# Two graph layers on one core: TensorE's register loads per couple of spans, and one branch per couple

## The chip, the core and the metric

The program runs on one core of a Trainium2 chip. The metric is the device time of that core in microseconds (us); the median over several executions is compared. Lower is better.

## The reference

There are 6250 nodes with 256 features, and 100000 edges sorted by their destination. The input is normalised per row, then two relational graph layers follow, a residual sum, a second normalisation and a mixture of 8 experts (top 2) with a residual sum. One graph layer is:

```
xs = x[src]
seg = dst * R + etype                          # R = 8 relations
sums = segment_sum(xs, seg, N * R)
mean = sums / max(cnt, 1)
out = x @ Wroot + b + einsum('nrd,rde->ne', mean.reshape(N, R, D), W)
```

The destinations are drawn as `6250 * u**2`, so the first nodes have many edges and the last ones few.

## The kernel before

**Blocks and spans.** The sorted edges are cut into 784 blocks of 128 edges. POOL gathers the source rows of one block per indirect DMA (L450) into a ring of 16 places, each with a high and a low half in float16 and a column of ones. The 49 tiles of 128 nodes are cut into 8 spans of 16 nodes (16 nodes x 8 relations = 128 rows of sums). Two spans are a couple, so a tile has 4 couples, numbered k = 0 to 3, and a layer has 196. The edges of a span touch at least one block; the program always takes two (its "first blocks") and, if they touch more, the further ones one by one.

**DVE** builds the 0/1 selection matrices: `sel` for the two first blocks of each span (L890), two couples ahead, and `sel_more` for every further block (L898), one couple ahead. It also takes the reciprocal of the counts (layer 0 alone), and the low halves of the means (L933). **ACT** writes the high halves of the means (L589) and copies transposed means out of PSUM (L561).

**TensorE** (PE) does, for every couple (function `couple`, L1258 and after), in this order: for both spans a wait for the rows and once for `sel`, then `add_block` (L1234, L1235: two matmuls each, high and low) for the two first blocks, then `more_sums` (L1237 to L1242: a branch, and if there are further blocks a loop over them, each with a wait for `sel_more`). Between these stand some of the products of the layer's weights with the means of the tile before (`product`, L1254, three matmuls a part, 18 parts a tile). At the end come 8 transposes of the means of the couple before (`turn`, L1246), which wait for DVE.

**What PE's sequencer does.** Where a block lies is known only on the chip. PE's own sequencer therefore loads numbers into registers and works out places and wait values from them. `load_meta` (L1225 to L1229) loads 20 numbers once a tile: first block and running count of further blocks, for 8 spans and a little more. The place of a block in the ring is `block & 15` and that is multiplied out to an address, for each matmul of `add_block`. A couple has two branches of its own (L1238), one per span, over the loop of further blocks.

```
1238                     with pe.If(upto > since):
1239                         with pe.Fori(0, upto - since) as i:
1240                             pe.wait_ge(more_ready[layer], since + i + 1)
```

**The order of the products.** A tile's 18 parts are spread over the couples k = 1, 2, 3 and the k = 0 of the next tile as 2, 6, 5 and 5. In k = 1 both stand at the couple's end, behind a wait for the last means of the tile (`means_in`).

**SyncE** (SP) passes on two kinds of events: a landed gather becomes `rows_ready` (L355), and a place in the ring of which PE has taken the last sum becomes `slots_free` (L362), for which POOL waits.

**Tiles.** `graph_tiles` writes out tiles 0, 1 and 48 and puts the others, in pairs, in a loop of 23 turns, so that on PE the code of 8 couples is the body of a loop (its backward branch is at L294). Behind the two layers, from about 2290 us on, comes the mixture of experts, which the change touches in nothing but the type of one small table.

## Time and profile before

| | |
|---|---|
| median of 3 runs | 3062.41 us (3062.01 to 3065.25) |
| the profiled execution: span, which is all of its own time that the page gives | 3064.4 us |
| PE busy | 2352.2 us (77%) |
| POOL busy | 1836.5 us (60%) |
| DVE busy | 1782.2 us (58%) |
| ACT busy | 1167.6 us (38%) |
| first and last tile of layer 0 begin on PE | 95.3 and 1174.2 us |
| first and last tile of layer 1 begin on PE | about 1197.1 and 2264.5 us |
| mean granted clock of TensorE | 0.879 |

"Busy" counts matmuls, copies and gathers. The instructions of a sequencer (register arithmetic, branches, loads of registers, semaphores) are not in it; they show as "issue", and with a q behind the engine's name (PEldq is PE's sequencer) in the view of one source line. A busy share of PE is no share of its peak, since the ends of matmuls overlap.

### The profile page before, as it was taken

To read this page: it belongs to the slowest core of one execution; us is meant where nothing else is said; L and a number is where in the kernel's file an instruction comes from. 1 tells how busy PE (TensorE), PEld (TensorE's weight loads), DVE (VectorE), ACT (ScalarE), POOL (GpSimd) and SP (SyncE) were. 2 spreads that over 40 slices of the span, in tenths; PEclk is the share of its full clock that TensorE was granted. 3 is DMA by queue.
4 is the path that set the end of the run, shared out by engine and by line. 5 is a ranking of instruction groups with operands and counts; after the bars stand their busy time and mean duration, and the time that the engine had idled before them with its cause. 6 is when DMAs were issued, how large, how long until landed. Compare 5 with 4: busy or idle time off the path is not lost.

```text
span 3064.4 us, 82720 instructions
## 1 busy us (share of the span) xinstructions
PE 2352.2 (77%) x19212; PEld 1776.0 (58%) x19213; DVE 1782.2 (58%) x4944; ACT 1167.6 (38%) x2306; POOL 1836.5 (60%) x1908
## 2 busy tenths in 40 slices
PE   1456777778888887456777888888987189999999
PEld 0123444555666775123445556667776178888888
DVE  7434445555566664333445555656666278877777
ACT  5001223334445553011223344455542165655554
POOL 1777777766666553777777777666536623333333
PEclk9556789999999998557899999999995599999999
DMA  7343333333333321333343444333335432322222
GB/s 244 100 130 105 108 108 108 109 101 99 97 94 93 90 88 58 106 99 115 115 119 118 123 122 125 112 113 111 106 110 192 146 123 86 100 72 72 72 72 61
DMA packets 164416, 331.14 MB, mean 108 GB/s; under 512 B 35518, under 2 KB 101786, under 8 KB 164216
## 3 DMA queue, kind: packets, MB, share of 16 engines
q0 software_dynamic: 90864, 245.38, 26.9%
q1 hardware_dynamic: 39608, 41.02, 4.5%
q10 hardware_dynamic: 33872, 43.92, 4.5%
q8 instruction: 27, 0.44, 0.1%
q14 instruction: 45, 0.37, 0.0%
HBM read 283.29 MB, written 49.07 MB: 108 GB/s over the span
## 4 chain that ended last, share of the span: by engine, by line
PE 48%; POOL 24%; issue 15%; DVE 7%; DMA 3%; DVEq 2%; ACT 1%; POOLq 0%; SPq 0%; ACTq 0%
POOL ring L450 20%; PE more_banks L1254 15%; PE sum_banks L1392 8%; PE sum_banks L1234 7%; PE sum_banks L1235 5%; PE sum_banks L1382 4%; PE more_banks L1382 4%; POOL lot_in L470 3%; PE more_banks L1246 3%; DMA ring<-table,row_tab 2%; DVE sel L890 1%; DMA out<-edge_work,lot_ids 1%; PE more_banks L1366 1%; DVEq L881 1%; DVE weights L1072 0%
## 5 line engine op out<-in xcount | busy, mean ns | idle before, releaser
L450 POOL DMA_INDIRECT ring<-table,row_tab x1568 | 1509.2, 963 | 703.8 <-issue 339.0
L1254 PE MATMUL more_banks<-weights,stage 128*128 128x256 f16 x5292 | 846.9, 283 | 7.8 <-ACT stage L561 4.5
L589 ACT ACTIVATE stage<-sum_banks,inv 128x256 f16<-128x256 f32 x784 | 327.4, 471 | 815.5 <-DVE inv L923 398.7
L1254 PEld LDWEIGHTS more_banks<-weights,stage 128*128 128x128 f16 x5292 | 502.4, 101 | 144.9 <-issue 71.6
L1234 PE MATMUL sum_banks<-ring,sel 128*128 x1568 | 449.3, 287 | 161.1 <-DVE sel L890 84.2
L898 DVE TENSOR_SCALAR sel_more<-lane,win_off,key_tab 128x128 f16 x780 | 268.8, 345 | 443.4 <-SPq L355 371.2
L1234 PE MATMUL sum_banks<-ring,sel_more 128*128 x780 | 244.3, 314 | 350.0 <-DVE sel_more L898 193.8
L890 DVE SCALAR_TENSOR_TENSOR sel<-lane,win_off,key_tab 128x256 f16<-128x256 f16 x792 | 349.4, 482 | 240.4 <-PE more_banks L1254 235.8
L1235 PE MATMUL sum_banks<-ring,sel 128*128 x1568 | 448.7, 287 | 0.0
L561 ACT ACTIVATE stage<-more_banks 128x1024 f16<-128x1024 f16 x392 | 402.7, 1027 | 15.1 <-PE more_banks L1246 14.9
L1234 PEld LDWEIGHTS sum_banks<-ring,sel_more 128*128 x780 | 78.4, 100 | 529.7 <-issue 524.9
L933 DVE SCALAR_TENSOR_TENSOR stage<-sum_banks,inv,stage 128x256 f16<-128x256 f32 x784 | 345.4, 479 | 25.8 <-issue 13.3
L1234 PEld LDWEIGHTS sum_banks<-ring,sel 128*128 128x128 f16 x1568 | 157.4, 100 | 266.5 <-issue 240.5
L489 POOL DMA_INDIRECT out<-edge_work,lot_ids x106 | 108.1, 1019 | 325.0 <-DVE edge_work L1160 308.7
L587 ACT ACTIVATE stage<-sum_banks 128x256 f16<-128x256 f32 x196 | 75.1, 383 | 591.3 <-DVE inv L923 302.1
L1235 PE MATMUL sum_banks<-ring,sel_more 128*128 x780 | 261.2, 336 | 0.0
L1246 PE MATMUL more_banks<-ident,stage 128*128 128x128 f16 x3136 | 257.3, 229 | 0.1
L665 ACT ACTIVATE stage<-sum_banks,edge_work,undo 128x256 f32<-128x256 f32 x212 | 113.0, 561 | 315.6 <-PE sum_banks L1382 294.1
L1246 PEld LDWEIGHTS more_banks<-ident,stage 128*128 128x128 f16 x3136 | 223.3, 103 | 14.0 <-DVE stage L933 1.2
L1392 PE MATMUL sum_banks<-weights,edge_work 128*128 128x256 f16 x1824 | 208.1, 275 | 7.5 <-DVE edge_work L1144 7.5
L920 DVE TENSOR_SCALAR inv<-sum_banks 128x2 f32 (+1 forms) x196 | 31.2, 159 | 290.6 <-PE more_banks L1254 276.1
L1392 PEld LDWEIGHTS sum_banks<-weights,edge_work 128*128 128x128 f16 x1824 | 179.5, 99 | 29.9 <-issue 8.4
(287 smaller groups left out, 2763.0 us busy)
## 6 DMA issues: line engine op xcount, KB each, us to landing
ring<-table,row_tab POOLq DMA_INDIRECT x1568
weights<-L_ffn_W ACTq DMA_DIRECT2D x96, 178.5 KB
stage<-L_ffn_W ACTq DMA_DIRECT2D x16, 1024.0 KB, 5.5
edge_work<-lot_in SPq DMA_DIRECT2D x54, 260.0 KB, 2.7
table<-edge_work SPq DMA_DIRECT2D x7, 896.0 KB, 4.4
table<-edge_work ACTq DMA_DIRECT2D x49, 128.0 KB
out<-acc SPq DMA_DIRECT2D x6, 1024.0 KB
acc<-x SPq DMA_DIRECT2D x6, 896.0 KB, 11.0
```

The lines of the kernel that those rows point to most:

```text
L450: pool.indirect_dma_start(ring_rows[:, b % RING, 0:2 * D], None, tables[layer], bass.IndirectOffsetOnAxis(row_tab[:, b:b + 1], 0)).then_in ...
L561: act.activation(means[:, par, :, :, 2 * k * WIN:(2 * k + 2) * WIN].rearrange("p q r (v n) -> p v (q r) n", v=2), ps_turn[slot].rearrange( ...
L589: act.activation(mean16[:, slot, h, 0:D], ps_sum[slot][h][:, 0:D], ACT.Copy, scale=inv[:, ds(c * 2 + h, 1)]).then_inc(mean_high[layer], 1)
L890: return v.scalar_tensor_tensor(sel[:, slot, h], lane16[:].unsqueeze(1).to_broadcast([P, 2, P]), win_off[:, ds(w, 1)], key_tab[:, ds(lo, 2 ...
L898: v.tensor_scalar(flat(sel_more[:, ds(block & (RING - 1), 1), :]), lane16[:], win_off[:, ds(w, 1)], key_tab[:, ds(block, 1)], ALU.add, ALU ...
L933: v.scalar_tensor_tensor(mean16[:, slot, h, D:2 * D], ps_sum[slot][h][:, 0:D], inv[:, ds(c * 2 + h, 1)], mean16[:, slot, h, 0:D], ALU.mult ...
L1234: pe.matmul(to[:, 0:D + 1], hot, flat(slot[:, :, D:2 * D + 1]), start=first, stop=last, skip_group_check=True)
L1235: return pe.matmul(to[:, 0:D], hot, flat(slot[:, :, 0:D]), start=False, stop=last, skip_group_check=True)
L1246: out = [pe.transpose(ps_turn[slot][:, (4 * h + q) * P:(4 * h + q + 1) * P], mean16[:, slot, h, q * P:(q + 1) * P], ident16[:]) for h in r ...
L1254: return [pe.matmul(ps_out[par], rows[:, xp * KD + k, :], w16[:, wp, k, r * D:(r + 1) * D], start=part == 0 and n == 0, stop=part == PARTS ...
L1382: ins = pe.matmul(hid_bank[c % 4], up_sb[slot][:, wp, k, c * P:(c + 1) * P], lotT[:, zp, k, :], start=k == 0 and (wp, zp) == PART_PAIRS[0] ...
L1392: ins = pe.matmul(bank[2 + h][:, 0:D], hidT[:, hp, c, h * P:(h + 1) * P], down_sb[slot][:, wp, c, :], start=c == 0 and (hp, wp) == PART_PA ...
```

## The change

TensorE no longer loads 20 numbers a tile. A new table `pe_row`, made once by DVE, holds six numbers per couple: for each span the two addresses in the ring of its first blocks, multiplied out, and in the two third places what the rows must have reached for both spans, and how many further blocks the couple has. PE loads these six at the start of every couple. If the couple has further blocks, a second load fetches six numbers of the old table, and an arm follows that does what was done before. Else a second arm does the first blocks of both spans with the products between, and has no further branch. The products are spread 5, 4, 4, 5 over k = 0 to 3, root parts first, and the wait for `means_in` moves from the end of k = 1 to the start of k = 2. On other engines: wait values that come from registers are masked (SP, DVE, PE), on ACT `relu_rows` comes from k = 2 to k = 3, before the transposed means, and on DVE `sums_out` goes from k = 1 to k = 2 and the bias sum from k = 2 to k = 1.

```diff
+    MASK = (1 << (BLOCKS + 3 * WINDOWS).bit_length()) - 1
+    PART_ORDER = [R * KD + k for k in range(KD)] + list(range(R * KD))
+    SHARES = (5, 4, 4, 5)
+    SPREAD = {4: (1, 1, 0, 1, 1), 5: (1, 1, 1, 1, 1)}
...
+        pe_row = sb("pe_row", [1, 6 * COUPLES], i32)
...
-                        sp.wait_ge(steps_done[layer], sp.snap(regs[s], donate=True, min_val=1, max_val=BLOCKS + 3 * WINDOWS))
+                        sp.wait_ge(steps_done[layer], sp.snap(regs[s], donate=True) & MASK)
...
+            for b in range(2):
+                link(v.tensor_scalar(places, lo, float(b), None, ALU.add))
+                link(v.tensor_scalar(places, places, RING - 1, None, ALU.bitwise_and))
+                link(v.tensor_scalar(pe_meta[0:1, :, :, b], places.rearrange("o (c h) -> o c h", h=2), float(PITCH), None, ALU.mult))
+            v.tensor_scalar(pe_meta[0:1, :, 0, 2], by_half[:, :, 1], 2.0, None, ALU.add)
+            v.tensor_tensor(pe_meta[0:1, :, 1, 2], more_half[:, :, 0], more_half[:, :, 1], ALU.add)
...
                 with v.If(upto > since):
+                    held = v.snap(lo & MASK)
                     with v.Fori(0, upto - since) as i:
...
-                        v.wait_ge(rows_ready[layer], block + 1)
+                        v.wait_ge(rows_ready[layer], held + i + 3)
...
+                def add_rows(to, hot, at, first, last):
+                    pe.matmul(to[:, 0:D + 1], hot, ring_row[:, ds(at + D, D + 1)], start=first, stop=last, skip_group_check=True)
+                    return pe.matmul(to[:, 0:D], hot, ring_row[:, ds(at, D)], start=False, stop=last, skip_group_check=True)
...
                 def more_sums(to, lo, since, upto):
                     with pe.If(upto > since):
+                        done = pe.snap(since & MASK)
                         with pe.Fori(0, upto - since) as i:
-                            pe.wait_ge(more_ready[layer], since + i + 1)
-                            block = (lo + i + 2).with_bounds(min_val=0, max_val=BLOCKS - 1)
-                            add_block(to, flat(sel_more[:, ds(block & (RING - 1), 1), :]), block, False, True).then_inc(steps_done[layer], 1)
+                            slot = pe.snap((lo + i + 2) & (RING - 1))
+                            pe.wait_ge(more_ready[layer], done + i + 1)
+                            add_block(to, flat(sel_more[:, ds(slot, 1), :]), slot, False, True).then_inc(steps_done[layer], 1)
...
+                    near = load_six("near", pe_row[0:1, ds(c * 6, 6)])
+                    at = [[pe.snap(near[3 * h + b], donate=True, min_val=0, max_val=(RING - 1) * PITCH) for b in range(2)] for h in range(2)]
+                    need, extra = (pe.snap(near[3 * h + 2], donate=True) for h in range(2))
...
+                    if k == 2 and age > 0:
...
                         pe.wait_ge(means_in[layer], t * STEPS)
+                    with pe.If(extra > 0):
+                        far = load_six("far", meta_row[0:1, ds(c * 4, 6)])
...
+                        for h in range(2):
+                            to = ps_sum[slot][h]
+                            pe.wait_ge(rows_ready[layer], (lo[h] & MASK) + 2)
+                            if h == 0:
+                                pe.wait_ge(sel_ready[layer], c + 1)
+                            add_rows(to, sel[:, slot, h, 0, :], at[h][0], True, False).then_inc(steps_done[layer], 1)
+                            if h == 0:
+                                some(0)
+                            add_rows(to, sel[:, slot, h, 1, :], at[h][1], False, True).then_inc(steps_done[layer], 1)
+                            if h == 0:
+                                some(1)
+                            more_sums(to, lo[h], mark[h], mark[h + 1])
+                            some(2 + h)
...
+                    with pe.Else():
+                        pe.wait_ge(rows_ready[layer], need & MASK)
+                        pe.wait_ge(sel_ready[layer], c + 1)
+                        for h in range(2):
+                            to = ps_sum[slot][h]
+                            add_rows(to, sel[:, slot, h, 0, :], at[h][0], True, False).then_inc(steps_done[layer], 1)
+                            some(3 * h)
+                            add_rows(to, sel[:, slot, h, 1, :], at[h][1], False, True).then_inc(steps_done[layer], 1)
+                            if h == 0:
+                                some(1)
+                                some(2)
...
+                    first = some(4)
```

## Rows read from the trace of the kernel before

**Rows 1.** The page's chain of work that ended last, shares of the span by engine.

```profile
PE 48%; POOL 24%; issue 15%; DVE 7%; DMA 3%; DVEq 2%; ACT 1%; POOLq 0%; SPq 0%; ACTq 0%
```

**Rows 2.** Busy time by stretch: us, PE, PEld, DVE, ACT, POOL, PEclk, DMA share, GB/s.

```profile
371.90:816.70 444.80, 346.86 (x2773) 240.41 (x2771) 239.34 (x705) 157.91 (x300) 319.46 (x335) 0.93 0.36 104
1493.50:1918.90 425.40, 339.65 (x2777) 240.35 (x2776) 225.38 (x566) 152.20 (x281) 321.72 (x335) 0.94 0.41 121
816.70:1197.10 380.40, 331.79 (x3186) 267.33 (x3184) 245.37 (x717) 199.49 (x380) 211.70 (x220) 1.00 0.29 86
1918.90:2287.80 368.90, 330.67 (x3199) 268.25 (x3197) 222.71 (x540) 191.34 (x354) 212.70 (x226) 1.00 0.36 107
```

**Rows 3.** POOL's gathers from 500 to 600 us: duration ns min/median/max, first and last start.

```profile
L450 POOL DMA_INDIRECT ring<-table,row_tab x81: 942/946/1217, 499.0 to 599.8; - x81
```

**Rows 4.** PE's instructions of eight tiles, 2156.3 to 2264.4 us, by source line; columns as above.

```profile
L1227 PEldq TENSOR_LOAD <-meta x8: 1358/1360/1362, 2156.3 to 2251.5; - x8
...
L1234 PEldq ALU_OP  x200: 36/36/36, 2157.9 to 2263.2; - x100
L1234 PEldq FUSED_REGOPS  x136: 41/60/84, 2158.0 to 2263.3; - x136
...
L1235 PEldq FUSED_REGOPS  x132: 37/40/42, 2158.1 to 2263.5; - x132
...
L1238 PEldq COMPARE_BRANCH  x64: 77/208/215, 2158.7 to 2263.6; - x64
...
L1278 PEldq ALU_OP  x64: 36/36/36, 2157.7 to 2262.7; - x64
...
L294 PEldq COMPARE_BRANCH  x4: 83/214/214, 2183.0 to 2264.3; - x4
```

**Rows 5.** Single tiles by stretch, columns as in rows 2: layer 1, layer 1, layer 0.

```profile
2156.30:2169.20 12.90, 11.79 (x121) 9.97 (x119) 7.95 (x20) 7.55 (x14) 7.52 (x8) 1.00 0.36 110
...
1979.80:1996.40 16.60, 14.57 (x135) 10.95 (x133) 9.80 (x24) 7.55 (x14) 11.13 (x13) 1.00 0.40 117
...
1061.50:1074.90 13.40, 11.79 (x121) 9.93 (x119) 9.06 (x27) 7.44 (x15) 7.69 (x8) 1.00 0.30 88
```

**Rows 6.** PE's load of four numbers in the mixture of experts, the whole span.

```profile
L1371 PEldq TENSOR_LOAD <-lot_meta x8: 331/333/339, 2448.6 to 3044.9; - x8
```

**Rows 7.** PE's entries into the loop of further blocks, 1493.5 to 1918.9 us.

```profile
L1239 PEldq MOVE  x129: 29/29/29, 1496.2 to 1915.6; - x129
```

**Rows 8.** The same from 1919 us to the layer's end.

```profile
L1239 PEldq MOVE  x34: 29/29/29, 1922.8 to 2276.5; - x34
```

**Rows 9.** What PE waited for from 371.9 to 816.7 us: total us, times, longest.

```profile
PE sum_banks L1234 <- issue: 42.6, 101, 0.7
PE sum_banks L1234 <- DVE sel L890: 26.0, 19, 1.6
PE sum_banks L1234 <- DVE sel_more L898: 23.2, 27, 1.2
```

**Rows 10.** The same from 1493.5 to 1918.9 us.

```profile
PE sum_banks L1234 <- issue: 39.9, 79, 1.6
PE sum_banks L1234 <- DVE sel_more L898: 19.2, 31, 1.0
PE sum_banks L1234 <- SPq L355: 16.2, 15, 1.6
```

**Rows 11.** What SP waited for from 371.9 to 816.7 us.

```profile
SPq L362 <- PE sum_banks L1235: 260.1, 215, 3.9
```

**Rows 12.** One of DVE's small operations on one partition, in order of time.

```profile
82.56 0.35 DVE L857 CAST meta<-weights 1x392 int32<-1x392 f32 x1
```

**Rows 13.** The page's DMA issues: a transfer from DRAM and its median us to landing.

```profile
edge_work<-lot_in SPq DMA_DIRECT2D x54, 260.0 KB, 2.7
```

More of the change, by code:

```diff
@@ L589, in tile_work @@
                             act.activation(mean16[:, slot, h, 0:D], ps_sum[slot][h][:, 0:D], ACT.Copy, scale=inv[:, ds(c * 2 + h, 1)]).then_inc(mean_high[layer], 1)
+                        if layer == 0 and k == 3 and age == 2:
+                            relu_rows(t - 2, par)
                         if age > 0 or k > 0:
@@ L596, in tile_work @@
                                 load_weights()
-                            if k == 2 and age == 2:
-                                relu_rows(t - 2, par)
                             if k == 3 and age == 2:
@@ L857, in _ @@
             v.tensor_copy(meta[0:1, 0:WINDOWS, 0], lo)
+            by_half = lo.rearrange("o (c h) -> o c h", h=2)
+            more_half = more.rearrange("o (c h) -> o c h", h=2)
+            places = span_rows[0:1, 5, :].bitcast(i32)
+            for b in range(2):
[4 more added lines that the diff above has]
+            v.tensor_tensor(pe_meta[0:1, :, 1, 2], more_half[:, :, 0], more_half[:, :, 1], ALU.add)
             v.tensor_copy(meta[0:1, 1:WINDOWS + 1, 1], upto)
@@ L881, in load_meta @@
                 v.load(regs, meta_row[0:1, ds(2 * w, 2 * count)])
-                lo = [v.snap(regs[2 * k], donate=True, min_val=0, max_val=BLOCKS - 1) for k in range(count)]
+                lo = [v.snap(regs[2 * k], donate=True) for k in range(count)]
                 return regs, lo, [v.snap(regs[2 * k + 1], donate=True, min_val=0, max_val=BLOCKS) for k in range(count)]
@@ L934, in tile_work @@
                                                    ALU.mult, ALU.subtract).then_inc(mean_low[layer], 1)
-                        if k == 1 and age == 2:
+                        if k == 2 and age == 2:
                             sums_out(t - 2, par)
@@ L1222, in _, with load_six @@
             loads = [0]
-            def load_meta(w):
+            ring_row = ring[:, :].bitcast(f16)
+            loads = [0]
+            def load_six(what, row):
                 loads[0] += 1
-                regs = [pe.alloc_register(f"pe_meta{loads[0]}_{k}") for k in range(2 * WPT + 4)]
-                pe.load(regs, meta_row[0:1, ds(2 * w, 2 * WPT + 4)])
-                lo = [pe.snap(regs[2 * k], donate=True, min_val=0, max_val=BLOCKS - 1) for k in range(WPT)]
-                return regs, lo, [pe.snap(regs[2 * k + 1], donate=True, min_val=0, max_val=BLOCKS) for k in range(WPT + 1)]
@@ L1231, in _ @@
-            for layer in range(2):
-                def add_block(to, hot, block, first, last):
-                    slot = ring_rows[:, ds(block & (RING - 1), 1), :]
-                    pe.matmul(to[:, 0:D + 1], hot, flat(slot[:, :, D:2 * D + 1]), start=first, stop=last, skip_group_check=True)
-                    return pe.matmul(to[:, 0:D], hot, flat(slot[:, :, 0:D]), start=False, stop=last, skip_group_check=True)
+                regs = [pe.alloc_register(f"pe_{what}{loads[0]}_{k}") for k in range(6)]
@@ new lines, in load_six, with release, add_block @@
+                pe.load(regs, row)
+                return regs
+            def release(regs):
+                for r in regs:
+                    pe.free_register(r)
+            for layer in range(2):
+                def add_rows(to, hot, at, first, last):
+                    pe.matmul(to[:, 0:D + 1], hot, ring_row[:, ds(at + D, D + 1)], start=first, stop=last, skip_group_check=True)
+                    return pe.matmul(to[:, 0:D], hot, ring_row[:, ds(at, D)], start=False, stop=last, skip_group_check=True)
+                def add_block(to, hot, slot, first, last):
+                    return add_rows(to, hot, (slot * PITCH).with_bounds(min_val=0, max_val=(RING - 1) * PITCH), first, last)
@@ L1274, in couple @@
                             pe.matmul(ps_root[slot][:, h, :], flat(rows16[:, ds(t, 1), (q + h) * P:(q + h + 1) * P]), ident16[:], start=True, stop=True, skip_group_check=True)
-                    for h in range(2):
-                        j = 2 * k + h
-                        to = ps_sum[slot][h]
-                        pe.wait_ge(rows_ready[layer], lo[j] + 2)
-                        if h == 0:
-                            pe.wait_ge(sel_ready[layer], c + 1)
-                        add_block(to, sel[:, slot, h, 0, :], lo[j], True, False).then_inc(steps_done[layer], 1)
-                        some(3 * h)
-                        add_block(to, sel[:, slot, h, 1, :], lo[j] + 1, False, True).then_inc(steps_done[layer], 1)
-                        if h == 0:
-                            some(1)
-                        more_sums(to, lo[j], mark[j], mark[j + 1])
-                        if h == 0:
-                            some(2)
-                    first.clear()
-                    if k == 1 and age > 0:
+                    if k == 2 and age > 0:
                         if age == 1:
@@ L1293, in couple @@
                         pe.wait_ge(means_in[layer], t * STEPS)
-                    some(4)
+                    with pe.If(extra > 0):
+                        far = load_six("far", meta_row[0:1, ds(c * 4, 6)])
+                        lo = [pe.snap(far[2 * h], donate=True) for h in range(2)]
+                        mark = [pe.snap(far[2 * h + 1], donate=True, min_val=0, max_val=BLOCKS) for h in range(3)]
+                        for h in range(2):
[11 more added lines that the diff above has]
+                            some(2 + h)
+                        release(far)
+                    with pe.Else():
[9 more added lines that the diff above has]
+                                some(2)
+                    release(near)
+                    first = some(4)
                     if first:
@@ L1319, in _ @@
                     weights_spread(1)
-                for n in range(PARTS):
+                for n in PART_ORDER[KD:]:
                     ins = product(0, n)[-1]
```

43 lines of the change are left out of this document (22 added, 21 removed).

## The prediction

> **What bounds the kernel now.** First the page's chain of what ended last [rows 1]: PE 48%, POOL 24%, and 15% "issue", time in which an engine waited for nothing that the profile shows. Nothing there says that DVE or ACT is short. The layers fill some 2190 of 3064 us, so I read them by stretch [rows 2]: tiles 4 to 23 of layer 0 and of layer 1, then tiles 24 to 48 of each. PE is never above 90% there. POOL at its quickest does 81 gathers in 100 us, 1.25 us each [rows 3]. Counted from the sorted destinations, tiles 4 to 23 hold 325 blocks, 406 us of gathering, and they take 445 and 425; from tile 24 on it is 227 blocks, 284 us, and 380 and 369. POOL bounds only the first four tiles of each layer.
>
> What is left is the "issue": PE's sequencer. [Rows 4] list its steps in eight tiles of 108.2 us. The seven kinds shown are 608 of 731 steps and last 47.3 us (8 loads of 1.36 us; 200 sums of 36 ns; 136 and 132 fused steps of 60 and 40 ns; 60 taken branches of 208 ns and 4 not taken of 77; 64 sums more; the loop's branches); 123 smaller ones of about 45 ns make 5.5. The remaining 55.4 us over 731 steps are 76 ns between two steps, and nearly all gaps are alike. So the sequencer is hardly ever held: it is the bound. Two tiles confirm it [rows 5]: 12.9 us without further blocks, 16.6 with four. One further block is 0.9 us, which its ten steps cost (0.46 us of records, 0.06 to 0.076 between each, less a taken branch for one not taken), while its two matmuls need 0.2.
>
> **The change, part by part.** I price a step at its record and 0.07 us.
>
> Load of six numbers: four last 0.333 us [rows 6], twenty 1.360 [rows 4], so 64 ns each and 0.46 for six; with the gap and the step for its address, 0.67 us. The load of twenty, 1.43 and half an address step, goes; per couple 0.38. The Trainium skill (Runtime: NRT & Kernel Launch, Instruction fetch mechanics) says about 200 ns per register; by that a load of six would be 1.2 us, and the sum below over 200 us instead of 75. The rows say a third of it, and they decide.
>
> A couple without further blocks: the two first blocks of each span no longer compute `block & 15` and `lo + 1`, six sums of 0.106, 0.64 us; one of three wait steps goes, 0.1; two taken branches become one, 0.28. It gains 0.64 + 0.1 + 0.28 + 0.38 and pays 0.67: **0.73 us less**, I take 0.75 since the address steps get a little shorter.
>
> A couple with further blocks: the same 0.64 and 0.38 go, and perhaps 0.08 in shorter address steps. It pays both loads, 1.34; the outer branch, not taken, 0.15; two more wait steps (two masks), 0.21; the mask of the running count in each span with further blocks, 0.15; and the jump over the other arm. No row shows an unconditional jump; the bounds are nothing and a taken branch, 0.28, and I take 0.2. The loop itself keeps its number of steps. **0.95 us more**, between 0.75 and 1.05.
>
> How many: counted from the input, 130 of a layer's 196 couples have further blocks: all 16 of tiles 0 to 3, all 80 of tiles 4 to 23 (129 loops are entered there [rows 7]), 34 of the 100 behind [rows 8].
>
> Tiles 4 to 23: 80 x 0.95 = 76 us a layer, less the waits that a later sequencer no longer meets. Layer 1 waits 35.4 us for `sel_more` and rows [rows 10]; half of it is overlapped with the sequencer's own gaps and stays, so +59, with +41 and +76 as ends. Layer 0 runs the same steps 19.4 us slower [rows 2], for DVE's selections come later there [rows 9], and that goes too: +40.
>
> Tiles 24 to 48: a tile without further blocks has now 11.8 us of PE busy in 12.9, and in layer 0 DVE has 9.1 and its own load of twenty, which stays [rows 5]. The sequencer would need 3 us less, but PE can give 1.0 (to about 12.1), layer 0 1.3 (to 12.5). Five tiles of that kind: -5 and -6. Nine with one such couple: -1.4 each, -13 a layer. Seven with two (+1.9 - 1.5): 0 and -3, waits included. Two with three: +4. One with four: +3. Sum -11 in layer 1, -15 in layer 0. The even spread of the products, and the wait for `means_in` put where it has long come, are in those floors; behind the last tile they save some 1.5 us a layer, -3.
>
> Tiles 0 to 3: gathers set the pace and cover most of 15 us; +3 a layer. If that cover were gone, +15.
>
> DVE's table: eight operations of about 0.35 us [rows 12], three in a row behind `link`, ahead of `setup_done`, for which PE waits. POOL has by then just filled the ring, so no cover: +3. The masks on SP, 0.1 us for each of 1568 blocks, lie before a wait that SP meets early (it waits 260 of 445 us for PE [rows 11]); cost nothing, and 157 us if SP were the bound. DVE's mask and the moved steps on ACT and DVE (0.42 and 0.47 us changing places) lie in DVE's idle time, a fifth to a third of each stretch [rows 2]: nothing; up to 0.5 us a tile, 45 us in all, if DVE were the bound. TensorE's clock: 0.93 to 0.94 of the 2.4 GHz level in tiles 4 to 23, where PE is busy 78% [rows 2]. It will be idler; I take nothing, up to +10.
>
> **The sum:** 59 + 40 - 11 - 15 - 3 + 6 + 3 = **+79 us**. The profiled span is 3064.4 us, 2.0 above the median; on the median 3062.4 + 78 gives **3140 us**.
>
> **The rivals.**
>
> *The heavy arm is covered (faster).* If the price of a couple with further blocks is under about 0.5 us, because arrivals and DVE, not the sequencer, set the pace of tiles 4 to 23, both stretches there add 0 to +10 and the light tiles still give 30 a layer: 3062 + 10 - 60, about 3010 to 3040. It turns at 0.55 us. For it: PE does wait for `sel_more` [rows 9, 10] and POOL is within 5 to 10% of its rate. Against: two tiles differ by just the steps of their loops [rows 5]. 0.19.
>
> *It cancels (no change).* Price 0.6, the light arm as forecast: within 6 us of now. 0.07.
>
> *The loop's code no longer fits (far slower).* The two arms write the first blocks and most products twice, for eight couples. Today the backward branch costs 214 ns, as a short one does [rows 4]. If each of 46 turns had to fetch its code anew, at about a landing from DRAM, 2.7 us [rows 13], it would be +124 on top: 3264. The Trainium skill, in the section named above, has a taken branch outside the fetched window wait for such a fetch; no run here shows it so far. 0.06.
>
> *It doesn't do what it says.* The second load might be in both arms; the diff excludes it. 0.
>
> **How the numbers follow.** The forecast, slower, has 0.68; its own range with the ends of the heavy price (0.75 and 1.05 us, 32 us over 160 couples down, 16 up), the waits (-35 to +35) and the clock is 3085 to 3190. Reaching down to the faster case until a tenth is left out, and up with the same: 3035 to 3190. A measurement of this kernel can tell 0.2%, 6 us, from no change. Slower 0.68 + 0.06 = 0.74, same 0.07, faster 0.19.
>
> **What would show it.** PE's load of six at about 0.46 us, 392 near and 260 far; tiles of four such couples at 20 us instead of 16.6, tiles without one near 12.3; PE's share in tiles 4 to 23 down to about 70%, waits for `sel_more` nearly gone; POOL slower than 1.25 us a block from tile 4 on. Wrong if tiles 4 to 23 stay at 425 us, if light tiles stay at 13, or if the backward branch is followed by microseconds of nothing.

## The result and the profile after

The changed kernel takes 3636.65 us (median of 4 runs, 3636.01 to 3637.02), the kernel before 3062.31 in the same comparison: a ratio of 1.187 (1.185 to 1.189). It is slower, as forecast, but by 574 us instead of 78, and far outside the range. The profiled span is 3634.7 us. TensorE's mean granted clock fell from 0.879 to 0.841 of the 2.4 GHz level.

The page's chain of what ended last, after:

```profile
PE 54%; issue 24%; DVE 9%; POOL 5%; DVEq 4%; DMA 1%; ACT 1%; POOLq 0%; SPq 0%; ACTq 0%
```

"Issue" rose from 15% to 24% and POOL fell from 24% to 5% [rows 1]. What POOL waits for says the same, with SP's queue passing on that PE is not done with a slot (294.4 us in the kernel before):

```profile
POOL ring L458 <- SPq L370: 942.4, 716, 4.0
```

The four stretches of rows 2, after (layer 0 and 1 of tiles 4 to 23, then of the tiles behind; in layer 1 the last tile is left out); columns as in rows 2:

```profile
423.20:1021.40 598.20, 391.59 (x2780) 261.11 (x2778) 239.91 (x706) 157.38 (x300) 308.04 (x326) 0.88 0.26 76
1809.20:2407.00 597.80, 399.15 (x2781) 266.86 (x2778) 225.35 (x566) 153.84 (x281) 308.10 (x326) 0.85 0.29 84
1021.40:1475.90 454.50, 352.59 (x3195) 279.59 (x3193) 246.24 (x717) 200.21 (x381) 208.61 (x220) 0.97 0.25 72
2407.00:2826.40 419.40, 325.01 (x2986) 257.10 (x2984) 212.15 (x513) 181.20 (x336) 207.88 (x221) 0.99 0.31 90
```

Tiles 4 to 23 are 153 and 172 us longer [rows 2], and both layers now take the same time: the pace has one cause. PE and DVE have the same instructions as before, and DVE the same busy time; PE's busy time is 45 and 60 us longer at the lower granted clock (0.88 and 0.85), but that is still only two thirds of the stretch. PE's sequencer shows the cause; the view of its source lines (count, duration in ns min/median/max, first and last start in us):

```profile
L1248 PEldq TENSOR_LOAD <-pe_row x392: 814/1155/1751, 98.9 to 2836.8; - x196
L1248 PEldq TENSOR_LOAD <-meta x260: 812/817/840, 100.0 to 2838.5; - x130
...
L1266 PEldq MOVE  x1170: 29/29/40, 101.8 to 2841.5; - x195
...
L302 PEldq COMPARE_BRANCH  x46: 76/216/218, 422.7 to 2825.9; - x46
...
L1414 PEldq TENSOR_LOAD <-lot_meta x8: 982/987/1002, 3014.5 to 3615.1; - x8
```

A load of six is 0.82 us where couples have an even number, 1.47 where odd (the median of 1155 lies between the two), and 0.817 for the second load. The forecast had 0.46. 652 loads take 665 us by their records, the 98 of before, at 1.36 [rows 4], took 133. The loop's MOVE is there 1170 times instead of 390: 390 entries and 780 iterations. The backward branch is as quick as before. Added up over PE's sequencer in layer 1, tiles 4 to 23: before, 3189 steps of 191.3 us and 234.1 us between them, 425.4 in all; after, 3639 steps of 345.1 us and 252.5 between them, 597.6 in all. That records and gaps add up to the stretch is true of any sequencer, busy or waiting. What tells is the mean gap: 73 ns before (80 in layer 0), 69 after in both layers, and only 36 gaps of layer 1 are above 0.12 us. So it is hardly ever held; nothing else sets the pace there. PE's waits say the same, in layer 1, tiles 4 to 23 (beside [rows 10]):

```profile
PE sum_banks L1257 <- issue: 156.3, 154, 2.3
PE sum_banks L1257 <- DVE sel_more L916: 4.4, 5, 0.9
```

Of the 172 us, 130 are loads (27.2 to 157.1), 24 other records, 18 gaps.

Ten of the runs below fell on chips on which the kernel before itself takes 3517 to 3521 us, not 3062, so each is compared only with runs of the same kind of chip.

### The profile page after: what moved, and what is told of

Read it like the earlier page. It is cut to its first block, busy times and chain, and to the rows that moved or that the text cites. A ratio compares the mean times of both kernels' runs of the same rounds, so it can differ in the third digit from the quotient of the medians.

```text
span 3634.7 us, 86880 instructions
## 1 busy us (share of the span) xinstructions
PE 2527.2 (70%) x19212; PEld 1852.9 (51%) x19213; DVE 1780.7 (49%) x4952; ACT 1170.2 (32%) x2306; POOL 1828.0 (50%) x1908
## 4 chain that ended last, share of the span: by engine, by line
PE 54%; issue 24%; DVE 9%; POOL 5%; DVEq 4%; DMA 1%; ACT 1%; POOLq 0%; SPq 0%; ACTq 0%
PE more_banks L1281 17%; PE sum_banks L1257 13%; PE sum_banks L1258 8%; PE sum_banks L1435 6%; DVE sel L907 3%; PE sum_banks L1425 3%; PE more_banks L1425 3%; POOL lot_in L478 3%; PE more_banks L1273 2%; POOL ring L458 2%; DVEq L916 1%; DVE sel_more L916 1%; PE sum_banks L1301 1%; DVEq L913 1%; DVE inv L938 1%
## 5 line engine op out<-in xcount | busy, mean ns | idle before, releaser
L1281 PE MATMUL more_banks<-weights,stage 128*128 128x256 f16 x5292 | 905.2, 298 | 1.8
L1257 PE MATMUL sum_banks<-ring,sel 128*128 x1568 | 467.5, 303 | 472.0 <-issue 322.1
L1281 PEld LDWEIGHTS more_banks<-weights,stage 128*128 128x128 f16 x5292 | 531.8, 106 | 144.6 <-issue 57.1
L1257 PE MATMUL sum_banks<-ring,sel_more 128*128 x780 | 261.8, 336 | 373.8 <-issue 252.2
L1258 PE MATMUL sum_banks<-ring,sel 128*128 x1568 | 468.0, 303 | 0.0
L916 DVE TENSOR_SCALAR sel_more<-lane,win_off,key_tab 128x128 f16 x780 | 254.7, 326 | 420.6 <-SPq L363 221.3
L1258 PE MATMUL sum_banks<-ring,sel_more 128*128 x780 | 283.2, 363 | 0.0
L1273 PE MATMUL more_banks<-ident,stage 128*128 128x128 f16 x3136 | 266.3, 234 | 0.7
L1273 PEld LDWEIGHTS more_banks<-ident,stage 128*128 128x128 f16 x3136 | 232.3, 106 | 19.7 <-issue 4.2
```

Source lines behind the costliest of these rows:

```text
L916: v.tensor_scalar(flat(sel_more[:, ds(block & (RING - 1), 1), :]), lane16[:], win_off[:, ds(w, 1)], key_tab[:, ds(block, 1)], ALU.add, ALU ...
L1257: pe.matmul(to[:, 0:D + 1], hot, ring_row[:, ds(at + D, D + 1)], start=first, stop=last, skip_group_check=True)
L1258: return pe.matmul(to[:, 0:D], hot, ring_row[:, ds(at, D)], start=False, stop=last, skip_group_check=True)
L1273: out = [pe.transpose(ps_turn[slot][:, (4 * h + q) * P:(4 * h + q + 1) * P], mean16[:, slot, h, q * P:(q + 1) * P], ident16[:]) for h in r ...
L1281: return [pe.matmul(ps_out[par], rows[:, xp * KD + k, :], w16[:, wp, k, r * D:(r + 1) * D], start=part == PART_ORDER[0] and n == 0, stop=p ...
```

## The experiments

**What a load costs: the list.** The first list of loads (e0) had no reader, and neither had the second load of six in e1. Both traces hold the changed kernel's 392 and 260 loads and no more; the added ones are in neither.

> Behind the end of PE's program this kernel loads 1 to 8, 12, 16 and 20 numbers from the table of spans, each three times, once from every one of four neighbouring starting places. Nothing else is changed, so the whole time stays that of the changed kernel plus the list. Theory A (groups of four): four numbers that start at a multiple of 16 bytes are read at once, each other number singly at about 245 ns. From an aligned start it expects 245, 490, 735, 333, 580, 820, 1060, 607 ns for 1 to 8 numbers and 1360 for 20; from the start one, two or three numbers on, 245 ns times the count throughout, so 980 for four, 1470 for six, 4900 for twenty. Theory B (my forecast's): a fixed part and 64 ns a number wherever it starts: 0.46 us for six everywhere, and the 0.82 and 1.47 us seen in the changed kernel come from something else there (the register address, other engines' traffic). Theory C: the start decides by a fixed extra, the same for every count.

> The changed kernel with the load of six numbers per couple made a second time, into registers that nobody reads; no number of the output changes. If the loads are the bound in PE's sequencer (theory A), each costs its record and the gap, 0.82 + 0.13 and 1.47 + 0.13 us by turns, 1.27 in the mean: 392 x 1.27 = 498 us if nothing covers any of it, about 450 with the waits that remain taken off: 4060 to 4140 us. If the time went into the two arms and their branches or waits (theory B), and the loads lie beside waits, under 100 us more: below 3740.

```diff
 near = load_six("near", pe_row[0:1, ds(c * 6, 6)])
+release(load_six("spare", pe_row[0:1, ds(c * 6, 6)]))
```

They took 3945.5 and 3967.4 us (one run each) beside 3517.1 for the kernel before. Both are the changed kernel on that chip, so their mean, 3956, give or take 11, is the base for e2 and e3. They say nothing for or against either theory. With a reader:

```diff
+for rep in range(3):
+    for start in range(4):
+        for count in (1, 2, 3, 4, 5, 6, 7, 8, 12, 16, 20):
+            pe.load(price, meta_row[0:1, 64 + start:64 + start + count])
+            at = (price[0] & 7)   # picks the place of a matmul of 64 columns
```

> Ahead of the layers PE loads 1 to 8, 12, 16 and 20 numbers from the table of spans, each three times from every one of four neighbouring starting places; one number of each load picks the place of a small matmul, so that the load is used (a list that nobody read left no load in the trace of the run before it). The whole time says nothing. Theory A (four numbers that start at a multiple of 16 bytes are read at once, each other singly at about 245 ns) expects from an aligned start 245, 490, 735, 333, 580, 820, 1060, 592, 850, 1110 and 1360 ns for 1 to 8, 12, 16 and 20 numbers; from a start one, two or three numbers on 245 ns times the count: 980 for four, 1470 for six, 4900 for twenty. Theory A2 (aligned fours inside an unaligned load are found): a load of eight from three numbers on would be 1 single, one four, three singles, about 1.3 us instead of 1.96. Theory B (a price per number wherever it starts): 64 ns each from every start, 0.46 us for six.

Rows of single loads: from the first starting place four, six, eight, then sixteen and twenty; from two numbers on four, six, twenty:

```profile
L1259 PEldq TENSOR_LOAD <-meta x1: 341/341/341, 101.1 to 101.1; - x1
L1259 PEldq TENSOR_LOAD <-meta x1: 825/825/825, 102.6 to 102.6; - x1
L1259 PEldq TENSOR_LOAD <-meta x1: 594/594/594, 105.0 to 105.0; - x1
L1259 PEldq TENSOR_LOAD <-meta x2: 1104/1230/1356, 107.1 to 108.4; - x2
L1259 PEldq TENSOR_LOAD <-meta x1: 1001/1001/1001, 136.0 to 136.0; - x1
L1259 PEldq TENSOR_LOAD <-meta x1: 1467/1467/1467, 138.8 to 138.8; - x1
L1259 PEldq TENSOR_LOAD <-meta x1: 4730/4730/4730, 152.0 to 152.0; - x1
```

Theory A holds, A2 and B fall; only the shortest loads are longer than A had them (one number 0.31 us instead of 0.245). From the first place the medians for 1 to 8, 12, 16, 20 numbers are 309, 547, 768, 333, 606, 828, 1061, 594, 855, 1104, 1356 ns: about 0.08 us and 0.255 for every whole four, 0.23 to 0.27 for each number left over. From each of the other three places all are 0.07 + 0.233 us a number: eight 1.93, twenty 4.73. An aligned four inside an unaligned load isn't found. My two points, 4 and 20, were both aligned and whole; the line between them holds only at multiples of four.

**The same six numbers, read otherwise.**

> The changed kernel with all PE loads of the layers made eight numbers long: those of odd couples start two numbers earlier, so that each starts at a multiple of 16 bytes; the numbers beside the six are dropped. More is read than before, and the same six are used. Theory A (groups of four aligned numbers are one read, others single): an aligned eight lasts 0.6 us, so each odd couple saves 0.87, each even one and each second load 0.21: 196 x 0.87 + 196 x 0.21 + 260 x 0.21 = 266 us less, less some 20 to 60 that the waits take back: 3370 to 3430 us. Theory B (a price per number): a third more for each load, 150 to 200 us more, about 3800. Theory C (the loads are not the bound): no change.

```diff
-regs = [pe.alloc_register(f"pe_{what}{loads[0]}_{k}") for k in range(6)]
+regs = [pe.alloc_register(f"pe_{what}{loads[0]}_{k}") for k in range(8)]
...
-return regs
+return regs[skip:skip + 6]
...
-near = load_six("near", pe_row[0:1, ds(c * 6, 6)])
+near = load_six("near", pe_row[0:1, ds(c * 6 - 2 * (k % 2), 8)], 2 * (k % 2))
-far = load_six("far", meta_row[0:1, ds(c * 4, 6)])
+far = load_six("far", meta_row[0:1, ds(c * 4, 8)])
```

```profile
L1248 PEldq TENSOR_LOAD <-pe_row x392: 3/592/988, 99.0 to 2912.1; - x196
L1248 PEldq TENSOR_LOAD <-meta x260: 2/590/1024, 99.8 to 2912.9; - x130
```

3756.2 us, 200 less than the 3956 of e0 and e1 (ratio to before 1.069, 1.066 to 1.072, against 1.125); theory A had 206 to 246 less. Reading a third more is faster; a price per number (B) and loads beside the path (C) are refuted.

> The changed kernel with its row of numbers for PE laid one number (4 bytes) further on, so that no load of six starts at a multiple of 16 bytes, even couples' no more than odd ones'. Theory A: all 392 last 1.47 us (none holds a whole aligned four that starts where it starts); the 196 even ones gain 0.65 us each, 128 us more at most, some 110 to 130: about 3755 us. If a load may find an aligned four inside itself (theory A2), a load of six that starts one number on (three single, then three) finds none, and one that starts three on would: even couples 1.47 and odd ones 0.25 + 0.33 + 0.25 = 0.82, and the time stays at 3637. Theory B (a price per number alone): no change, 3637, with both kinds as now.

```diff
-pe_row = sb("pe_row", [1, 6 * COUPLES], i32)
+pe_row = sb("pe_row", [1, 6 * COUPLES + 1], i32)   # and every use one number on
```

```profile
L1248 PEldq TENSOR_LOAD <-pe_row x392: 18/1469/1809, 99.2 to 3236.0; - x196
```

4070.6 us (one run), 114 more than 3956, or 103 to 125 with the two runs of the base. 196 loads grew by 0.65 us, 128 us: eight to ten tenths of it show in the time. A2 and B, which had no change, fall again.

> The changed kernel with the load of six numbers per couple made twice, the places taken from the first and the other two numbers from the second, so that both are used. (The run in which nobody read the second one shows 392 loads, not 784: it was the changed kernel once more.) If the loads are the bound in PE's sequencer (theory A), 392 x (0.82 or 1.47, 1.145 in the mean, + 0.19 for gap and address step) = 523 us if nothing covers any of it, 430 to 523 with the waits that remain: on a chip where the kernel before takes 3062 us 4070 to 4160, a ratio of 1.33 to 1.36. If the time went into the two arms and their branches (theory B): under 100 us more, ratio below 1.22.

```diff
+again = load_six("again", pe_row[0:1, ds(c * 6, 6)])
-need, extra = near[2], near[5]
+need, extra = again[2], again[5]
```

784 loads now, 4133.2 us (one run), 1.349 of the kernel before: 494 to 497 us more for 523 us of loads and gaps. The load is on the path nearly everywhere; in the 24 light-to-mixed tiles behind (layer 1) the stretch grew by 133 us for 96 x 1.335 = 128.

**The masks and the loop.**

> The kernel before with the masks on awaited values alone (PE, DVE and SP), and the table of lots in 16 bits: no second arm, no new loads. PE gets two more sums per couple (0.106 us each with the gap) and one per entered loop: 784 x 0.106 + 390 x 0.106 = 124 us at most over both layers, of which a part lies beside waits in layer 0's early tiles: +50 to +120 us by the theory that PE's sequencer is the bound all through, ratio 1.02 to 1.04. The rival, that the masks fall into gaps: ratio 1.00 to 1.005.

```diff
-pe.wait_ge(rows_ready[layer], lo[j] + 2)
+pe.wait_ge(rows_ready[layer], (lo[j] & MASK) + 2)
...
+done = pe.snap(since & MASK)
-pe.wait_ge(more_ready[layer], since + i + 1)
+pe.wait_ge(more_ready[layer], done + i + 1)
```

3230.7 us, ratio 1.054 (1.053 to 1.056): 166 us, above the 124 that I gave as most. I had counted one mask per entered loop. The trace has two steps more in every iteration:

```profile
L1242 PEldq MOVE  x1170: 29/29/38, 98.9 to 2439.0; - x195
...
L1243 PEldq ALU_OP  x780: 36/36/36, 99.1 to 2439.2; - x195
L1243 PEldq FUSED_REGOPS  x780: 41/41/41, 99.2 to 2439.3; - x195
```

The value written outside the loop is computed again in each turn: a copy of the counter, the mask, the sum, where one fused step had done; at the entry there is no mask. By themselves the added steps would be 83 us for the masks of the waits for rows and 148 us for the loops, 231; 166 show in the time, so the theory that the sequencer is the bound all through is too strong for this kernel, and the rival, that they fall into gaps, is refuted. Tiles 4 to 23 of layer 1 grew from 425.4 to 471.4 us:

```profile
1585.00:2056.40 471.40, 360.66 (x2773) 247.82 (x2771) 226.29 (x565) 152.61 (x280) 311.05 (x327) 0.91 0.36 107
```

> The kernel with the masks alone (ratio 1.054 to the kernel before) and, beside them, the change's other free-standing parts: the new order of the 18 products with its even spread, the wait for the means in front of couple 2, the moved steps on ACT and DVE, the new ends of the layers. My forecast's theory: a few us a layer, 5 to 30 in all, better spread and shorter ends: ratio 1.044 to 1.053. Rival 1: the order changes nothing that PE's sequencer sees, 1.054. Rival 2: the even spread makes PE wait for turns and means that came in time before: above 1.06.

The diff is the change's own order of products, its waits for the means, the steps moved on ACT and DVE and the ends of the layers, on top of the masks. 3219.3 us, ratio 1.050 (1.049 to 1.052): 11 us faster than the masks alone, as the forecast's theory had it. No run separates the order from the moved steps and the ends. The granted clock in tiles 4 to 23 of layer 1 is 0.94 instead of 0.91.

**A load per tile.**

> The changed kernel with PE's numbers of four couples loaded at once, 24 per tile from a multiple of 16 bytes, and the second load of a couple with further blocks made eight numbers long. Theory A: 98 loads of about 1.63 us take the place of 392 of 0.82 or 1.47 (-289 us), 294 address steps and gaps go (0.19 us each, -56), and the second loads go from 0.817 to 0.592 (-58): 400 us at most, 310 to 390 less after the waits that come back: ratio to the kernel before 1.06 to 1.09 instead of 1.187. If the branches and arms, not the loads, made most of the loss (theory B), the ratio stays above 1.12.

```diff
-near = load_six("near", pe_row[0:1, ds(c * 6, 6)])            # per couple
+near = load_some("near", pe_row[0:1, ds(t * 24, 24)], 24)     # per tile
-far = load_six("far", meta_row[0:1, ds(c * 4, 6)])
+far = load_some("far", meta_row[0:1, ds(c * 4, 8)], 8)
```

```profile
L1248 PEldq TENSOR_LOAD <-meta x260: 585/592/606, 100.5 to 2505.4; - x130
L1248 PEldq TENSOR_LOAD <-pe_row x98: 1612/1618/1645, 98.6 to 2495.9; - x98
...
1628.60:2140.60 512.00, 368.65 (x2773) 253.83 (x2772) 225.97 (x565) 152.36 (x280) 309.13 (x326) 0.90 0.33 98
2461.30:2473.50 12.20, 11.08 (x120) 9.97 (x117) 8.22 (x21) 7.51 (x14) 7.56 (x8) 1.00 0.38 115
```

3307.4 us, ratio 1.080 (1.078 to 1.081), 329 us less than the changed kernel with everything else in place, within theory A's 310 to 390. The last row is a tile without further blocks, cut 3 us behind its first load. From first load to first load five of them average 12.5 us (layer 1), where the kernel before had 13.1 and the changed one 13.5.

> The kernel with one load of 24 a tile (ratio 1.080, 243 us over the kernel before) with the loop over further blocks written over the awaited number itself: its start is masked once on entry, so that the move and the mask in each of the 780 iterations go, 10 steps instead of 12 with two matmuls among them. Theory (each step of PE's sequencer is on the path, 0.09 to 0.1 us with its gap): 780 x 0.19 = 148 us at most, 80 to 148 with the waits that come back: ratio 1.031 to 1.054. Rival (the steps lie beside waits for the selections): less than 30 us, ratio above 1.07.

```diff
-with pe.Fori(0, upto - since) as i:
-    slot = pe.snap((lo + i + 2) & (RING - 1))
-    pe.wait_ge(more_ready[layer], done + i + 1)
+shift = pe.snap(lo - since + 1)
+with pe.Fori((since & MASK) + 1, upto + 1) as j:
+    pe.wait_ge(more_ready[layer], j)
+    slot = (j + shift) & (RING - 1)
```

3244.2 us, ratio 1.059 (1.057 to 1.061): 63 us, where the two steps in 780 iterations had been priced at 148. Neither theory's range held it. Tiles 0 to 3 of layer 0 became 25 us shorter, tiles 4 to 23 of the two layers 15 and 11. The price was wrong, not the path: the edit also adds steps. In tiles 4 to 23 of layer 1 two steps go in each of 165 iterations, but one more comes at each of 129 entries, 201 less in all (3519 to 3318), and the fused steps of the ring's place got longer. Records went from 265.4 to 266.7 us, the time between them from 246.5 to 234.1: together just the 11 us.

**One arm or two.** Both kernels load 24 and 20 numbers at the head of a tile.

> As the kernel with one load of 24 a tile (ratio 1.080), but the numbers of the heavy arm too are loaded once per tile, 20 of them, instead of 8 in each of 260 couples; the two arms stay. By the loads' prices 260 x (0.592 + 0.19) = 203 us go and 98 x (1.36 + 0.07) = 140 come: 63 us less over all, but unevenly: tiles 4 to 23 lose 4 x 0.78 - 1.43 = 1.7 us each, tiles without further blocks gain 1.4 each where PE and DVE leave room. Ratio 1.055 to 1.07. If the second load in the heavy arm was covered by waits: 1.08 or above.

> As the kernel with two arms and both loads per tile, but without the branch per couple and the arm for couples without further blocks: each span tests for further blocks itself. Heavy couples save the outer branch and the jump over the other arm (0.15 + 0.24 us, 260 of them: 100 us), light ones pay two taken branches and one more wait and mask instead of one taken branch (0.28 + 0.2 us, 132 of them: 63 us). If the sequencer is the bound and the price of a branch is what the traces show: 20 to 40 us less than with two arms, gain in tiles 4 to 23 (80 x 2 x 0.39 = 62 us) and loss behind them. If the light arm is worth more than its branch costs (what the change was built for): slower than with two arms by 20 us or more.

```diff
-with pe.If(extra > 0):
-    far = load_some("far", ..., 8)
+far = load_some("far", meta_row[0:1, ds(t * 16, 20)], 20)      # both, per tile
...
-with pe.If(extra > 0): ... the first arm
-with pe.Else(): ... the second arm
+... the first arm alone                                       # v2 only
```

3380.5 (ratio 1.103, 1.101 to 1.105) and 3329.1 us (1.086, 1.084 to 1.088). The first is a miss: 73 us slower than v1, where 27 to 74 faster was expected. Tiles 4 to 23 of layer 1 gained 17 us, but the 24 behind lost 43, for loads that are 8 us longer there. Three rows of v3, the stretch behind and two of its light tiles:

```profile
2175.10:2573.80 398.70, 326.42 (x2990) 269.19 (x2989) 211.16 (x512) 182.45 (x336) 209.96 (x221) 0.92 0.33 95
2532.90:2546.80 13.90, 11.59 (x122) 10.42 (x122) 8.36 (x21) 7.58 (x15) 7.53 (x8) 1.00 0.38 111
2561.00:2576.50 15.50, 13.25 (x122) 11.47 (x122) 8.32 (x21) 7.69 (x15) 4.21 (x7) 0.89 0.21 44
```

Two things are to be seen. At the full clock the tile is 13.9 us instead of 12.2, by about the added load of 1.43. And in the other the mean clock is 0.89, the same matmuls take 13.25 instead of 11.59 us, and the tile 15.5. The same time cut finer shows where the clock goes:

```profile
2559.80:2561.80 2.00, 0.00 (x0) 0.00 (x0) 1.52 (x5) 1.22 (x2) 0.00 (x0) 1.00 0.37 61
2563.80:2564.80 1.00, 1.00 (x7) 0.71 (x5) 0.00 (x0) 0.00 (x0) 0.23 (x1) 0.50 0.22 29
2566.80:2573.80 7.00, 7.00 (x77) 6.37 (x75) 4.22 (x11) 5.08 (x9) 0.00 (x0) 1.00 0.24 63
```

The two loads, 1.62 and 1.36 us, run from 2558.2 to 2561.4 us. PE stands still for 2.2 us from 2559.8. From 2563.3 on, 1.3 us after it has taken up work again, its granted clock is at the lower of its two levels, 1.2 GHz, for 3.4 us. Of the last 11 tile heads of v3, with pauses of 2.2 to 3.1 us, six are followed by such a fall; the pause's length doesn't tell which. In v1, with 1.6 us of loads at the head and pauses of 0.7 to 1.5 us, the five light tiles are all at 1.00. The light arm did not pay either: one arm is 51 us faster, and faster in every stretch, also behind tile 24 (384.8 us against 398.7) where 63 of 96 couples take the light one. By the prices 20 to 40 us were expected, as a gain in tiles 4 to 23 and a loss behind, so the sign came true and the reason did not: behind tile 24 of layer 1 the sequencer with two arms has fewer steps (1929 against 2116) and 12 us less of records, but stands 25 us longer between them.

> As the kernel with two arms and 24 + 20 numbers at the head of a tile (ratio 1.103), but the arm for couples without further blocks waits for the rows of each span by itself, with one mask and one wait more. If the light arm's wait for both spans' rows ahead of its first matmul is what makes two arms 52 us slower than one: 30 to 50 us less, ratio 1.086 to 1.093. If it isn't: 132 couples with two steps more, +0 to +26 us, ratio 1.103 to 1.11.

> As the kernel with two arms and 24 + 20 numbers loaded at the head of a tile (ratio 1.103; light tiles 14.8 us in layer 1, 15.8 in layer 0), but each pair of couples loads its own 12 + 12. The loads grow from 2.98 to 4 x 0.856 = 3.42 us a tile, and two more address steps with gaps come, 0.4: 0.8 us a tile. If every us of loading costs its time wherever it stands: +60 to +80 us, ratio 1.12 to 1.13, light tiles 15.5. If a long stretch without a new matmul costs more than two short ones, because PE runs dry in it and is then itself the bound (lump theory): light tiles back to 13.3 to 14.3 us, 20 to 60 us less: ratio 1.083 to 1.096.

> As the kernel with one load of 24 a tile, the second loads in the heavy arm and the cheaper loop (ratio 1.059), with the 24 split in 12 per pair of couples: 1.71 instead of 1.62 us of load, and 0.2 for one more address step and gap: +0.3 us a tile. Sum theory: +20 to +28 us, ratio 1.066 to 1.068. Lump theory: the 1.6 us were already bridged for the most part in light tiles (12.6 us), so at most 10 to 20 us less: ratio 1.053 to 1.056.

> The kernel with masks and the new order of products (ratio 1.050), with the loop over further blocks written over the awaited number itself, so that its move and mask in each of 780 iterations go. No load is added anywhere. Where the loads were there, the same edit gave 63 us (25 of them in tiles 0 to 3, 26 in tiles 4 to 23); here the sequencer is less loaded: 45 to 90 us less, ratio 1.021 to 1.036. Rival (the two steps are covered by waits here): less than 20 us, above 1.043.

> The kernel with two arms and 24 + 20 numbers at the head of a tile once more, beside the one that loads them by pairs of couples, on the same chip. On a chip where the kernel before takes 3062 us: 3380 again, ratio 1.103. On one where it takes some 3520 us: if the light arm's wait for both spans costs 30 to 50 us, some 3835 to 3855 (v9, without it, took 3803 there); if it costs nothing, 3780 to 3805.

> The same with both loads by pairs of couples. Sum theory (each us of loading costs its time wherever it stands): 60 to 80 us more than the kernel run beside it. Lump theory (a long stretch of loading at the head of a tile lets PE run dry, two short ones are partly bridged): 20 to 60 us less than it. On the chip of its first run it took 3802 us.

```diff
-pe.wait_ge(rows_ready[layer], need & MASK)                     # v9, light arm
+pe.wait_ge(rows_ready[layer], (lo[h] & MASK) + 2)              # per span
...
-near, far = 24 and 20 numbers per tile                         # v7
+near, far = 12 and 12 numbers per pair of couples
```

On chips of the other kind: v3 again 3798.6, v7 3802.3 and 3800.7, v9 3803.0 us, with intervals of the ratio between 1.077 and 1.085 that all overlap. So the light arm's early wait doesn't cost the 30 to 50 us of its theory, and it isn't why two arms are slower. Loads by pairs hold 0.8 us a tile more, 80 us, and cost nothing net: neither the sum nor the theory that short stretches are faster gave that, though about 80 us were won back somewhere. v8 took 3685.8 us (ratio 1.048, 1.044 to 1.052) and b2 3609.6 (1.027, 1.023 to 1.031). On this kind of chip ratios are smaller throughout (v3 1.080 instead of 1.103), and v4 and b1 did not run there; so what the split and the cheaper loop add to v8 and b2 stays open. b2 is the nearest to the kernel before and still slower: no version tried beats it.

## Why the prediction was right in sign and wrong in size

**The bound: right.** PE's sequencer sets the pace, and more purely after the change: the mean gap between two steps is 69 ns, the waits for `sel_more` in tiles 4 to 23 of layer 1 fell from 19.2 to 4.4 us.

**The load of six: the step that failed.** "Four last 0.333 us, twenty 1.360, so 64 ns each and 0.46 for six". The straight line came from two whole, aligned loads. Measured: 0.82 aligned, 1.47 unaligned, since leftover and unaligned numbers cost 0.23 us each. In tiles 4 to 23 that alone is 80 x (1.145 - 0.46) + 80 x (0.817 - 0.46) = 83.5 us a layer; over both layers 392 x 0.685 + 260 x 0.357 = 361 us. The tile of layer 1 with four such couples (16.6 us before [rows 5], forecast 20) takes 24.9: 4 x (0.95 + 0.685 + 0.357) = 8.0 us more, measured 8.3. I had the warning in hand: the Trainium skill (Runtime: NRT & Kernel Launch, Instruction fetch mechanics) gives about 200 ns per register, by which a load of six is an estimated 1.2 us. This case's unaligned loads lie a sixth to a fourth above it (0.233 us a number, 1.47 us for six); its whole fours, 64 ns a number, lie far below, and from those alone I dismissed it, gave it no chance among the rivals, and put what it would do at "over 200 us", where 0.74 us more for each of 652 loads is over 480. The pitch of six numbers, 24 bytes, sets every second couple on a start that isn't a multiple of 16 bytes.

**"The loop itself keeps its number of steps": wrong.** It has two more, 165 x 0.19 = 31 us in tiles 4 to 23 of a layer, 148 in all; b0 shows masks and loop together at 166 us, v4 gets 63 back.

With these two, my own sum seems to come out: tiles 4 to 23, 40 + 83.5 + 31 = 154.5 and 59 + 83.5 + 31 = 173.5 us, measured 153 and 172. That is closer than it deserves, and partly luck. The mask once per entered loop, 0.15 us a couple and 12 us a layer in my price, isn't in the trace; small terms make it up. The address steps of the first blocks got 1 us shorter and not 6, the jump over the other arm is 0.17 us and its gap, 0.24 where I took 0.2 (3 us), and the waits that went away are 13 and 32 us by the mean gap (73 and 80 ns to 69, over 3188 steps), where I had 17 and 36. The jumps are the slower half of this row, 80 of 169 ns beside 80 branches not taken of some 75:

```profile
L1306 PEldq COMPARE_BRANCH  x160: 72/126/169, 1810.0 to 2405.9; - x160
```

Behind tile 23, 100 near and 34 second loads and 34 iterations add 69 + 12 + 6 = 87 us in layer 0 to my -15, which makes 72; in layer 1, without its last tile, 84 to my -11, 73. Measured +74 and +74.

**Tiles without further blocks: the saving is real, the loads ate it.** Forecast 12.1 and 12.5 us (layer 1, layer 0). From one tile's first load to the next one's, the five average 13.5 and 14.4, in the kernel before 13.1 and 13.8. With one load of 24 a tile (v1) they are 12.5 and 13.0, 0.6 and 0.8 us under the kernel before, where I had 1.0 and 1.3.

**Tiles 0 to 3: wrong.** I had gathers cover most of 15 us. They became 48 and 37 us longer. The 191 iterations a layer stand there, more than in the twenty tiles behind, and I had priced none of their steps: with the loads, 392 steps more, 69 us with their gaps. And the sequencer was near its bound there too: the kernel before has 1892 steps with mean gaps of 80 and 90 ns, so it was held for 20 and 39 us only, and that is all the cover there was.

**The rivals.** Code that no longer fits: refuted, the backward branch stays at 216 ns and the next step follows within 0.1 us in all 46 turns, as before; no run shows a wait for a fetch. The covered heavy arm and the even balance: refuted by tiles 4 to 23. **Clock:** "nothing, up to +10". In tiles 4 to 23 it went from 0.93 and 0.94 to 0.88 and 0.85, with little cost there, since the gaps of the sequencer leave room for no more than some 4 us of being held; where PE is nearly the bound, as in v3's light tiles, each fall costs 1.6 us.

**Table of lots in 16 bits: left out of the sum.** Four such numbers take 0.987 us instead of 0.333 [rows 6], on every engine that reads them. From the start of the last tile to the end the kernel grew by 9 us; b0, with the same table, shows 3 of them.

**DVE's table: right.** The first tile begins at 98.9 instead of 95.3 us, forecast +3.

**The order of products and the tails:** 11 us with the moved steps (b1), forecast a few and 3.

Together, from runs on one kind of chip: masks and loop steps +166, order -11; v1's cheap load, its second loads and the two arms, less the premultiplied places, +88; the loads of six in their stead, +329. That is 572 of 574 us; each is a difference along one chain of kernels, so the sum is no test, but each share is measured.

What stays open: why two arms are slower than one; no run separates the branch, the jump and the matmuls' place in the program, and no trace shows what holds the sequencer there.

## What to carry to other kernels

Where a sequencer is the bound, lay out what it loads in whole groups of four 32-bit numbers that start at a multiple of 16 bytes: six numbers at a pitch of 24 bytes cost 0.82 and 1.47 us, eight aligned ones 0.59. Don't price a third length by a line through two lengths that are both whole and aligned; a list of single loads shows the steps between them. And count the steps of a loop in the built program when a value that it awaits changes its form.

## What the runs showed of the hardware that I had not expected

A load's price has steps: a fixed 0.07 to 0.08 us, aligned fours at 0.255 us, everything else at about 0.233 us a number, with no credit for an aligned four inside an unaligned load. Four 16-bit numbers take 0.987 us, as four unaligned 32-bit ones do (1.00).

TensorE's clock fell from 2.4 to 1.2 GHz for 3.4 us shortly behind 2.2 us without a matmul (v3), and a light tile's matmuls took 13.25 us instead of 11.59; other tiles with pauses as long kept it.

Two kinds of chips: the kernel before takes 3062 us on one and 3517 to 3521 on the other. In the changed kernel PE's sequencer there (e1) stands still for 0.64 to 0.76 us 299 times and for 1.3 to 1.45 us 51 times between two steps; on the first kind 7 and 8 times. That is 280 us of the 330 by which the run is longer. No run shows what it waits for.
